# Graph kernel: the order of POOL's indirect DMAs around the picks, and the edge weights of the last sum pair by pair

## The reference, cut to what matters

```python
def _L0_gnn_ref(...):
    def scan_fn(x, p):
        m = x[src] @ W.T + b
        s = x[dst] @ W.T + b
        logit = m @ Wa[:, :HIDDEN].T + s @ Wa[:, HIDDEN:].T
        a = jnp.exp(jax.nn.leaky_relu(logit, negative_slope=0.2))
        n = jax.ops.segment_sum(a, dst, num_segments=n_nodes)
        h = jax.nn.relu(x / jnp.where(n == 0.0, 1.0, n))
        x = _rmsnorm(h + x, nw, nb)
        y = jax.nn.relu(x @ hW.T + hb)
        x = _rmsnorm(x + y, hnw, hnb)
        return (x, None)
...
def _L1_gnn_ref(...):
    e = el[src] + er[dst] + rel_w[etype]
    e_max = jax.ops.segment_max(e, dst, num_segments=n)
    e_exp = jnp.exp(e - e_max[dst])
    denom = jax.ops.segment_sum(e_exp, dst, num_segments=n)
    a = e_exp / denom[dst]
    return jax.ops.segment_sum(a[:, None] * nfeat[src], dst, num_segments=n)
...
def _L2_gnn_ref(...):
    def _graph_conv(h, src, dst, n, W_root, W_rel, b):
        agg = jax.ops.segment_sum(h[src], dst, num_segments=n)
        return h @ W_root.T + agg @ W_rel.T + b
    h = jax.nn.relu(_graph_conv(x, src, dst, n, W1_root, W1_rel, b1))
    return jax.nn.relu(_graph_conv(h, src, dst, n, W2_root, W2_rel, b2))
...
def _L3_gnn_ref(x, edge_index, edge_weights):
    messages = x[src] * edge_weights[:, None]
    return jax.ops.segment_sum(messages, tgt, num_segments=x.shape[0])
...
x = _layernorm(x + _L0_gnn_ref(...)); x = _layernorm(x + _L1_gnn_ref(...))
x = _layernorm(x + _L2_gnn_ref(...)); x = _layernorm(x + _L3_gnn_ref(...))
```

## Time and profile before

| | us |
|---|---|
| median of 3 runs (lowest, highest) | 4675.79 (4675.2, 4680.14) |
| span of the profiled execution | 5324.4 |
| PE busy in it | 3948.7 (74%) |
| DVE busy in it | 3635.2 (68%) |
| ACT busy in it | 1932.1 (36%) |
| POOL busy in it | 890.3 (17%) |

### The profile page before, as it was taken

The page is one execution under the profiler, slowest core; times in us unless marked ns, Lnnn a source line. Parts: engine busy times, 40 slices in busy tenths (PEclk is TensorE's granted clock), DMA queues, the critical chain, the costliest instruction groups (busy, mean ns, idle before and its releaser), DMA issues.

```text
span 5324.4 us, 227772 instructions
## 1 busy us (share of the span) xinstructions
PE 3948.7 (74%) x103291; PEld 3188.9 (60%) x103291; DVE 3635.2 (68%) x4577; ACT 1932.1 (36%) x2437; POOL 890.3 (17%) x810
## 2 busy tenths in 40 slices
PE   5540555327349247489999999979999979999997
PEld 4430445227348137356777777769989956666665
DVE  6872336316627535778889888865555599999997
ACT  6100101100010010056666666646556445455543
POOL 0566332460330421221010000000000000000000
PEclk9875577558659558689999999989989979999998
DMA  6641033205206105211111111135445300000000
GB/s 171 207 133 30 1 105 108 55 11 159 87 3 182 34 20 150 63 46 56 57 60 59 56 61 58 54 131 177 160 151 179 129 8 10 10 10 11 10 9 17
DMA packets 240238, 404.47 MB, mean 76 GB/s; under 512 B 110258, under 2 KB 167860, under 8 KB 239524
## 3 DMA queue, kind: packets, MB, share of 16 engines
q1 hardware_dynamic: 213928, 383.16, 23.0%
q0 software_dynamic: 25472, 10.79, 1.0%
q10 hardware_dynamic: 184, 0.08, 0.0%
HBM read 287.89 MB, written 110.03 MB: 75 GB/s over the span
## 4 chain that ended last, share of the span: by engine, by line
PE 65%; issue 11%; DVE 11%; another core or an unknown queue 4%; POOL 2%; ACT 1%; DMA 1%; SPq 0%; DVEq 0%; ACTq 0%
PE psum L1125 18%; PE psum L1098 15%; PE psum L1165 12%; PE psum L928 11%; PE psum L1086 3%; POOL gath L626 2%; DVE space L1655 1%; PE psum L884 1%; PE psum L1174 1%; PE psum L896 1%; PE psum L870 1%; DVE space L1435 1%; PE psum L1009 1%; DVE V L1420 1%
## 5 line engine op out<-in xcount | busy, mean ns | idle before, releaser
L782 ACT COPY space<-psum 128x784 f32<-128x784 f32 x1184 | 964.6, 815 | 751.8 <-PE psum L1098 689.3
L928 PE MATMUL psum<-table,space 128*128 128x56 bf16 x24300 | 738.8, 189 | 479.2 <-issue 415.7
L1098 PE MATMUL psum<-space 64*128 64x49 bf16 x56832 | 983.7, 184 | 108.1 <-issue 73.7
L1098 PEld LDWEIGHTS psum<-space 64*128 64x128 bf16 x56832 | 840.1, 94 | 345.5 <-issue 199.1
L1125 PE MATMUL psum<-space,X 128*64 128x256 f32 x7252 | 1029.9, 394 | 5.0 <-issue 2.4
L928 PEld LDWEIGHTS psum<-table,space 128*128 128x128 fp8e4 x24300 | 691.8, 97 | 524.9 <-issue 508.9
L1302 DVE TENSOR_REDUCE space<-psum 128x1512 f32 (+1 forms) x300 | 519.1, 1733 | 562.3 <-remote 308.3
L1655 DVE TENSOR_TENSOR space<-space 128x2352 bf16<-128x2352 bf16 x592 | 814.6, 1376 | 0.0
L1647 DVE TENSOR_TENSOR space<-space,V 128x2048 bf16<-128x2048 bf16 x592 | 720.8, 1218 | 0.0
L1165 PE MATMUL psum<-space 128*128 128x192 bf16 x7252 | 626.6, 247 | 11.1 <-ACT space L815 11.1
L1165 PEld LDWEIGHTS psum<-space 128*128 128x128 bf16 x7252 | 593.5, 98 | 36.4 <-issue 36.1
(11 more groups left out here) (286 smaller groups left out, 2976.5 us busy)
## 6 DMA issues: line engine op xcount, KB each, us to landing
space<-adj_d SPq DMA_DIRECT2D x148, 784.0 KB, 4.3
space<-onehots SPq DMA_DIRECT2D x240, 432.0 KB
adj_d<-space SPq DMA_DIRECT2D x222, 192.0 KB, 2.3
onehots<-space SPq DMA_DIRECT2D x60, 432.0 KB
space<-digit_rows SPq DMA_DIRECT2D x60, 378.0 KB
adj_d<-space SPq DMA_DIRECT2D x74, 208.0 KB, 1.9
space<-cw_d SPq DMA_DIRECT2D x37, 160.0 KB, 2.2
cw_d<-space SPq DMA_DIRECT2D x4, 1184.0 KB
```

Of the source, the lines that this page charges most:

```text
L782: nc.scalar.copy(A[:, h, :, b * P:(b + 1) * P].rearrange("p a (w s) -> p w a s", w=2)[:, :, :, c:c + UC], psum[:, 2 + 2 * (k % 2):4 + 2 * ...
L928: mm = nc.tensor.matmul(pb[(h % 2) * NBK + b][:, t * HI:(t + 1) * HI], rows[:, h, c:c + P].bitcast(FP8), table[:, r, :], start=(r == 0), s ...
L1098: mm = nc.tensor.matmul(psum[:, 2 + 2 * (k % 2) + w, c * NB:(c + 1) * NB], ohlo[lo:hi, ring, col // 2, :, col % 2], ohw[lo:hi, ring, r, co ...
```

## The change

- Chunks 0 to 3 of picks 1 to 4 are no longer straight code: the first loop now covers chunks 0 to 43, since MID goes from 40 to 44. The straight chunks with the carry are 44 to 47.
- From layer 1 on `scatter_heads` waits until five chunks of the pick are done.
- The 74 gathers of the records move to the ends of picks 1, 2 and 3 (`SPREAD`: 24, 24 and 26), behind a wait for 53 done chunks and ahead of the gather of ends.
- The gathers of the weights in layers 1 and 2, their split on DVE and their DRAM copy go. The second sum takes its weights as the first does: POOL two gathers, PE a transpose, DVE five instructions for each pair (`weights_of_pair(n, ...)`, `turn_weights(n, d)`). `cw_d` keeps the codes alone, once.
- `codes` moves from layer 1 to layer 3, `relations` from layer 3 to layer 1; its sum stays in SBUF and isn't stored and loaded again.
- The first sum's 49 single columns come two a pair.

```diff
-MID = 40
+MID = 44
...
+SPREAD = [(0, 24), (24, 48), (48, NRB)]
...
             def scatter_heads(n):
 
                 pool.wait_ge(spread_ready, n + 1)
+                if n:
+                    pool.wait_ge(pick_psum, n * NCH + OR + 1)
...
+            def weights_of_pair(n, d):
+
+                table = ew_pad.rearrange("(c e) -> c e", e=KC) if n else scans_d.rearrange("(c e) a -> c (e a)", e=KC)
+                if d >= 2:
+                    pool.wait_ge(pair_psum, n * NDB + d - 1)
+                elif n:
+                    pool.wait_ge(pair_psum, NDB)
+                for b in range(2):
+                    nc.gpsimd.indirect_dma_start(out=w_pair[:, d % 2, b * KC:(b + 1) * KC], out_offset=None, in_=table,
...
             for k in range(LAYERS):
                 scatter_heads(k)
                 if k == 1:
-                    records(NRB // 2, NRB)
-                if k == 2:
-                    weights_of_edges(NRB // 2, NRB)
-                gather_ends(k, k + 1)
-                if k == 0:
                     pool.wait_ge(rec_stored, 48)
                     pool.wait_ge(half_moved, 160)
-                    records(0, NRB // 2)
-                if k == 1:
-                    weights_of_edges(0, NRB // 2)
+                if k:
+                    pool.wait_ge(pick_psum, k * NCH + MID + 2 * OR + 1)
+                    records(*SPREAD[k - 1])
+                gather_ends(k, k + 1)
             scatter_heads(LAYERS)
...
-                for j in range(7 * (d - 1), 7 * d) if 1 <= d <= NB // 7 else ():
+                for j in range(2 * (d - 1), min(2 * d, NB)) if d else ():
...
-                for h in range(OR):
-                    pe.wait_ge(oh_loaded[h], 16 * ((k - 1) * (NCH // OR) + 1))
-                    pe.wait_ge(pick_read, k * NCH - 1 + h)
-                    chunk_from(ohr, h)
...
-                with pe.Fori(1, MID // OR) as i:
+                with pe.Fori(0, MID // OR) as i:
                     for h in range(OR):
                         next_chunk(i, h)
...
-                    if n == 0 and k == MIXED + 1 and D + 2 < NDB:
-                        turn_weights(D + 2)
+                    if k == MIXED + 1 and D + 2 < (n + 1) * NDB:
+                        turn_weights(n, D + 2 - n * NDB)
...
-                if k == 2:
-                    weights()
-                if k == 3:
-                    nc.vector.memset(xin[:, NB - 1, :], 0.0).then_inc(xin_zero, 1)
-                    relations()
...
-                    if n == 0 and more and t == 0 and mix:
-                        weights_of_pair(i, 1 - h, 5 * h + 5)
+                    if more and t == 0 and mix:
+                        weights_of_pair(n, i, 1 - h, 5 * h + 5)
```

More of the change, by code:

```diff
@@ L193, in gnn @@
         junk = VF[:, 1400:1400 + TF]
-        relF = reset[:, :]
         def view(at, n, dt=F32):
@@ L255, in share @@
             return v if dt == F32 else v.bitcast(dt)
+        rel_sum = share(0, TF)
+        etyI = share(TF, TF, I32)
+        rel_of = share(2 * TF, TF)
         ohb = share(0, OR * CH * P // 4, U8).rearrange("p (h e) -> p h e", h=OR)
@@ L483, in _ @@
                 if k == 1:
[L484 to L488, removed]
-                if k == 2:
[L490 to L493, removed]
                     sp.dma_start(etyI, ety_pad.rearrange("(p t) -> p t", t=TF)).then_inc(ety_loaded, 16)
                 if k == 3:
-                    sp.wait_ge(rel_w_ready, 1)
-                    sp.dma_start(rel_d, rel_sum).then_inc(tile_saved, 16)
+                    sp.wait_ge(code_read, CODES)
+                    for which, tile in ((0, loT), (1, hiT)):
+                        sp.dma_start(cw_d[:, :, which * P:(which + 1) * P].rearrange("d p x -> p d x"),
+                                     tile.rearrange("p (d x) -> p d x", x=P)).then_inc(codes_stored, 16)
             whole, tail = node_dram(x_in)
@@ L658, in _ @@
             for d in range(NDB):
[L659 to L664 removed]
+                weights_of_pair(0, d)
                 if d == 1:
                     pool.wait_ge(sums_stored, 16)
[L667 removed]
+                for j in range(2 * (d - 1), min(2 * d, NB)) if d else ():
                     nc.gpsimd.indirect_dma_start(out=gath[:, j:j + 1], out_offset=None, in_=sums_d,
                                                  in_offset=bass.IndirectOffsetOnAxis(ap=ends[:, j:j + 1], axis=0)).then_inc(sums_gathered, 16)
+            for d in range(2):
+                weights_of_pair(1, d)
             for h in range(2):
@@ L675, in _ @@
             nc.gpsimd.memset(xT[F:P, :], 0.0).then_inc(acc_zero, 1)
+            for d in range(2, NDB):
+                weights_of_pair(1, d)
         @block.scalar
@@ L1035, in codes @@
                 pe.wait_ge(code_read, CODES)
-            def weights():
-                for q in range(NWT):
-                    pe.wait_ge(weight_rows[q], 16 * (min(8 * q + 8, NRB) - 8 * q))
-                    if q >= 4:
-                        pe.wait_ge(wt_split, q - 3)
-                    for j in range(4 * q, min(4 * q + 4, NDB)):
-                        mm = nc.tensor.transpose(pb[q % 4][:, (j - 4 * q) * P:(j - 4 * q + 1) * P], wrow[:, j * P:(j + 1) * P], ident[:, :])
-                    mm.then_inc(wt_psum, 1)
-                pe.wait_ge(wt_split, NWT)
             pe.wait_ge(bb_copied, 4)
@@ L1116, in pair @@
                         if k == 0:
-                            if n == 0 and 2 <= D + 1 < NDB:
+                            if 2 <= D + 1 - n * NDB < NDB:
                                 pe.wait_ge(pair_step, 5 * (D + 1) + 1)
@@ L1556, in _ @@
                 if k == 1:
+                    relations()
+                if k == LAYERS - 1:
+                    nc.vector.memset(xin[:, NB - 1, :], 0.0).then_inc(xin_zero, 1)
                     dve.wait_ge(rec_rows, 16 * NRB)
@@ L1704, in weighted_sum @@
                 twice(n)
-                if n == 0:
-                    for h in range(2):
-                        weights_of_pair(0, h, 5 * h)
+                for h in range(2):
+                    weights_of_pair(n, 0, h, 5 * h)
                 pair(n, 0, 0, None, mix=False, put=False)
```

105 lines of the change are left out of this document (33 added, 72 removed).

## The result

The changed kernel takes 4702.81 us (median of 4 runs, 4701.44 to 4704.94), the kernel before 4677.97 us in the same comparison (4675.2 to 4680.78). The ratio is 1.0056 with a 95% interval from 1.0044 to 1.0069: **24.8 us slower**. The forecast was 4707.

The account below looks back on a forecast made before the run. It took the profile's stall as almost absent from the runs, and PE as waiting for DVE at step 0 in the second sum. 30.8 + 2.9 - 3 = +31 on 4675.8 gave 4707 us, range 4640 to 4735.

Parts of the forecast that it names:

- Standstills hardly in the runs: Picks, tails, first weighted sum: PE's and DVE's stalls belong almost wholly to the profiled execution, 618 of 648.6 us.
- the prediction's 618: Stall in the profile, in us: 419 in four picks, 141 in three tails, 58 in the first weighted sum.
- picks of 140 us: Sign in the profile after: picks this long would mean loops are immune to the stall, and rival 1 gains.
- rival 1: Picks and tails: the stall is in the runs too and loops escape it; faster, about 4627 us; chance 0.16.
- Second sum, 0.88 us a pair: Five added DVE instructions at step 0 make PE wait at step 1: 0.88 us over 35 pairs, 30.8 us.
- The first two pairs' weights, 2.9: Ahead of the second sum, DVE's work on two pairs' weights: 2 x 1.45 = 2.9 us added.
- Layer 2, -3: Layer 2's tail loses its split of the weights on DVE: between 0 and -6 us, taken as -3.
- Records, codes and relations at nothing: Pick ends and tails: moved records are covered, codes and relations change places between layers 1 and 3; 0 us.
- Chunks into the loop at nothing: Chunks 1 to 4 of a pick go into the loop: same 4860 matmuls, no wait added, 0 us.
- rival 3: Picks 1 to 4: slower scatters make the heads late, 15 us in each pick, 4765 us; chance 0.06.
- the lower bound +3: Second sum: if DVE's idle time takes all the pairs' added work, only 2.9 us are left.
- Rival 2: Second sum: DVE's spare time, 1.9 us a pair, swallows the weights; no change, 4676 us; chance 0.14.

Follow-up runs that it names:

- e10_before_third: The kernel before, unchanged, recorded a third time: span 4675.1 us.
- e8: The kernel before with all three edits of the picks (chunks 0 to 3 in the loop, MID 44, scatter behind chunk 5): 4669.74 us, 0.9991.
- e9: The kernel before with only chunks 0 to 3 put in the loop: 4671.16 us, 0.9991 of the kernel before.
- e4: The changed kernel with chunks 0 to 3 straight, MID 40 and no wait ahead of the scatter: 4702.13 us, 1.0054 of the kernel before.
- e2: The changed kernel with the second sum's five DVE instructions per pair spread over steps 0, 1 and 4: 4677.11 us, 1.0006 of the kernel before.
- e1: The kernel before, unchanged, recorded a second time: span 4682.6 us.

## Why the prediction was right, point by point

- **Standstills hardly in the runs: right.** The sum 5324 - 618 = 4706 stood 30 us off the runs, and two fresh recordings have picks of 142 to 146 us. Beside the third recording the 649 us lie in the picks (397), the tails (179), between pick 4 and the second sum (66) and ahead of pick 1 and at the end (7), so nothing of them is left for the runs: the prediction's 618 had the picks too high (419) and the tails too low (141). The forecast 139.6 for an undisturbed pick was 2 to 7 us short. What I drew from it for the other trace was wrong: I took the standstills for what a recording always adds to back-to-back DMAs on POOL, and so expected a span of 5200 to 5250 us with standstills at other places. It was 4703. The step that failed is "the stall belongs to the profiled execution" read as "to every one"; one recording could not tell. I had also named "picks of 140 us" as a sign for rival 1, and that sign deceives too: e10_before_third has them in straight code.
- **Second sum, 0.88 us a pair: right in mechanism and size.** PE waits 0.80 us at step 1, the pair goes from 26.56 to 27.42 us. 35 x 0.86 = 30.1; the sum grew by 25.0, because the 35 pairs of the kernel before are 5.7 us longer together than 35 x 26.56 (single pairs of up to 28.3 us), and those of the changed kernel only 0.8 longer than 35 x 27.42. The trace shows why: in the changed kernel an odd gap of PE falls into the wait behind it. PE in the pair that starts at 3693.11:

```profile
3695.88 0.20 PE L1067 MATMUL psum<-space 64*128 64x49 bf16 x2 [0.27 <-issue]
...
3697.46 0.80 PE L1067 MATMUL psum<-space 64*128 64x49 bf16 x48 [0.36 <-DVE space L1603]
```

  Ahead of step 1 it loses some 0.45 us, then waits 0.36 us instead of 0.80, and the pair takes 27.43 us like the others.
- **The first two pairs' weights, 2.9: right** (+3.0 from the first sum to the second).
- **Layer 2, -3: right** (-2.1; 136 to 139 us in the seven recordings with the change, 140 to 142 in the four without).
- **Records, codes and relations at nothing: mis-sized.** Layer 1's tail lost 5.5 to 7.9 us (4 to 5 beside e8 and e9, whose layer 1 is that of the kernel before and whose tails took 146.3 and 147.3), and layer 3's won nothing back. I had the records end some 8 us after the pick; they ended 24 to 26 us after it, for two reasons. They began 126.9 to 127.3 us after the pick's start, not 115.5: I took 53 chunks at 2.18 us and left out the waits around the carry, which stand before chunk 53 and for which the same prediction had 8.9 us. And I priced a record at 1.24 us; the 24 of layer 1 took 39.4 us instead of 29.8, since DVE's scans and logits hold POOL. And I called the swap even without asking when the edge types are loaded: of a step that moves, its DMA counts too.
- **Chunks into the loop at nothing: mis-sized the other way**, by some 4 us in the recordings (4.2 less than in the third recording, 10.7 less than in the second). That the runs gain by it is not shown: e8 and e9 are at the edge, e4 shows nothing.
- **The total missed by 6 us**, a fifth of the forecast move. The second sum's 25.0 in place of 30.8 is nearly all of that; that layer 1's loss and the picks' gain, neither of them forecast, nearly cancel is luck.
- **Slips in the working:** by its own terms rival 3 begins at 1.48 us a scatter ((95.9 - 10.9 - 2) / 56), not 1.40, and its four picks make 60 us, not 58; and the lower bound +3 is 4679, not 4690. None of them bears on the result.
- **Rivals.** Rival 1 is ruled out as a cause of the result by e4 and e8: the loops are worth some 5 us. Rival 2 is ruled out by the pair's 27.42 us; with e2 it becomes clear that it was a question of place: DVE's spare time does swallow the work at steps 1 and 4. Rival 3 didn't occur: no wait for the heads appears in a pick, and POOL's scatters kept their pace under DVE's reductions (in pick 1 the 56 take 52.45 us of work, 0.94 each).

## What to carry to other kernels

When two engines hand work to each other through a short ring, an added instruction is not priced by the engine's idle share but by the slack at the step where it is put: here 1.45 us cost 0.86 at one step and nothing when spread over three. Before explaining a profile, hold its span against the runs; where they differ by a tenth, record again, since both the standstills and what seems to cause them may belong to one execution. A swap of two pieces of work is only even if their loads and the engines they hold in passing are moved with them.

## What the runs showed of the hardware

**DVE holds POOL's indirect DMAs, by kind of instruction.** A DMA that takes 0.95 us on POOL took 2.67 beside DVE's pair of relations instructions (1.06 and 1.84 us), 4.09 beside a scan of 3.59 and 5.72 beside an instruction of 5.09, but 0.93 in the middle of a reduction from PSUM. The Trainium skill ("SBUF — State Buffer", section "Who interferes with whom") says that VectorE and GpSimd share a pair of ports under an exclusive lock, which some kinds of VectorE instructions take and a reduction does not; the rows of the reduction and the others agree in this. Of `tensor_tensor` the section also tells that a probe saw it stall no DMA; the instruction of 5.09 us is one, with both inputs in SBUF, and beside it the DMA took 5.72, so here the measurement decides.

**Code that PE meets for the first time is fed in pieces.** PE at the start of pick 1, the kernel before (third recording), then the changed one:

```profile
541.79 12.42 PE L928 MATMUL psum<-table,space 128*128 128x56 bf16 x398 [1.78 <-DVE table L1297]
555.36 3.54 PE L928 MATMUL psum<-table,space 128*128 128x56 bf16 x126 [1.15 <-issue]
559.49 3.38 PE L928 MATMUL psum<-table,space 128*128 128x56 bf16 x124 [0.59 <-issue]
563.03 52.66 PE L928 MATMUL psum<-table,space 128*128 128x56 bf16 x1944 [0.17 <-issue]
```

```profile
541.61 10.94 PE L914 MATMUL psum<-table,space 128*128 128x56 bf16 x324 [2.06 <-DVE table L1266]
552.72 78.49 PE L914 MATMUL psum<-table,space 128*128 128x56 bf16 x2916 [0.17 <-issue]
```

In the kernel before, matmuls 1 to 324 are the straight chunks and 325 to 648 the loop's first turn. The gaps of 1.15 and 0.59 us stand in that first turn, after matmuls 398 and 524, and not in the straight chunks. The first turn takes 10.9 us, with PE at a granted clock of 1.00, the later ones about 8.7; in the twelve picks with straight chunks (e1, e10, e4) it takes 9.7 to 13.1. In the changed kernel the first turn takes the straight chunks' place at the pick's start: it takes 11.1 us, where the straight ones took 10.4 (in both the first 3.7 us are at a granted clock of 0.50 and 0.51, the level of 1.2 GHz, after PE had waited some 2 us), and the second turn is already at 8.75. In e9, where POOL's scatters run beside the first chunks as in the kernel before, the second turn takes no more (8.71 to 8.75), so the scatters are not the cause. The 648 matmuls from the start take 21.1 us in the first (541.79 to 559.49 + 3.38) and 19.8 in the second (541.61 to 552.72 and 324 at 26.9 ns): half as much code is new in it. The Trainium skill ("Runtime: NRT & Kernel Launch", section "Instruction fetch mechanics") speaks of blocks of 256 instructions; 124 to 126 matmuls with as many weight loads are 248 to 252, which agrees. Its advice to prefer unrolled code isn't borne out here: the loop was not slower in any recording.
